# Layer 0's second context chunk as one 128-row operand; layer 1's normalisations on ScalarE with GpSimd's powers shared by two batches

## What is computed

```python
x = x + tanh(g_xattn[0]) * L0_xattn(ctx, layernorm(x), mask, ...)   # 4 heads of 64, keys from context and latents
x = x + tanh(g_ffn[0])   * L0_ffn(layernorm(x), ...)                # 8 experts, the best 2, and a shared one
x = x + tanh(g_xattn[1]) * L1_xattn(layernorm(x), ctx, ctx, ...)    # one head of 256
x = x + tanh(g_ffn[1])   * L1_ffn(layernorm(x), ...)                # 8 experts, the best 1
# L0_xattn: kv = concat([layernorm(ctx) @ Wkv.T, layernorm(latents) @ Wlkv.T]); softmax(q k) v @ Wo.T + bo
# L1_xattn: softmax((x Wq + bq) (ctx Wk + bk)^T) (ctx Wv + bv)
```

## Time and profile before

| | us |
|---|---|
| median of 3 runs | 1222.96 |
| lowest and highest run | 1221.63, 1227.02 |
| the profiled execution: its own time | 1228.26 |
| its span, first to last instruction | 1226.5 |

### The profile page before, as it was taken

The page is one execution under the profiler, slowest core; times in us unless marked ns, Lnnn a source line. Parts: engine busy times, 40 slices in busy tenths (PEclk is TensorE's granted clock), DMA queues, the critical chain, the costliest instruction groups (busy, mean ns, idle before and its releaser), DMA issues. The chain is left out here.

```text
span 1226.5 us, 30069 instructions
## 1 busy us (share of the span) xinstructions
PE 1052.9 (86%) x8055; PEld 811.7 (66%) x8056; DVE 742.9 (61%) x2369; ACT 568.7 (46%) x1310; POOL 449.0 (37%) x549
## 2 busy tenths in 40 slices
PE   3899999999999971999999999956878888179996
PEld 2687777777777751777777777745666767146664
DVE  5467777777777755344444443334788887445664
ACT  3466666666666640444444444422444444023332
POOL 3445666566665533000000000014577674312222
PEclk9799999999999975999999999977999999589999
DMA  4113221122211112354444443333743331444441
GB/s 135 32 36 107 78 70 57 60 74 76 83 57 45 46 69 86 87 129 126 126 125 128 128 99 83 84 97 109 232 137 119 102 119 52 121 98 105 111 111 50
DMA packets 153537, 116.26 MB, mean 95 GB/s; under 512 B 87695, under 2 KB 141249, under 8 KB 153218
## 3 DMA queue, kind: packets, MB, share of 16 engines
q1 hardware_dynamic: 112082, 57.46, 17.8%
q10 hardware_dynamic: 30816, 28.63, 7.9%
q0 software_dynamic: 10576, 29.41, 7.0%
HBM read 51.82 MB, written 45.92 MB: 80 GB/s over the span
## 5 line engine op out<-in xcount | busy, mean ns | idle before, releaser
L1458 PE MATMUL e_first<-w_high,e_z_cols 128*128 x824 | 175.4, 315 | 20.9 <-DMA e_z_cols<-z_rows 20.5
L1557 DVE SCALAR_TENSOR_TENSOR e_hidden<-e_first,e_act_out 128x352 f32<-128x352 f32 x103 | 54.0, 524 | 165.4 <-ACT e_act_out L1503 165.4
L1189 PE MATMUL a_out<-a_v_ones,a_probs 128*128 128x65 f32 x1024 | 140.2, 281 | 0.0
L1189 PEld LDWEIGHTS a_out<-a_v_ones,a_probs 128*128 128x128 f32 x1024 | 126.5, 194 | 15.1 <-issue 15.1
L1674 POOL IOTA a_first_numbers<- 128x2 int32 x1 | 0.1, 124 | 339.8 <-POOLq L70 339.8
L522 POOL DMA_INDIRECT z_rows<-r_z_halves,r_slot_idx x96 | 96.5, 1005 | 65.9 <-issue 32.7
L1458 PEld LDWEIGHTS e_first<-w_high,e_z_cols 128*128 128x128 f16 x824 | 81.0, 98 | 56.9 <-issue 21.3
L1562 DVE TENSOR_TENSOR e_hidden_low<-e_hidden_cols,e_hidden_high 128x384 f16<-128x384 f32 (+1 forms) x142 | 84.2, 593 | 48.9 <-ACT e_hidden_high L1512 48.2
L831 ACT ACTIVATE a_probs<-a_scores,a_latent_bias,a_k_scales 128x256 f32<-128x256 f32 x128 | 65.4, 561 | 99.5 <-PE a_scores L1175 62.1
L1503 ACT ACTIVATE e_act_out<-e_first 128x352 f32<-128x352 f32 x103 | 47.8, 464 | 136.2 <-PE e_first L1458 136.2
L1458 PE MATMUL e_first<-w_low,e_z_cols 128*128 x412 | 96.0, 315 | 0.0
(11 more groups left out here) (335 smaller groups left out, 2818.7 us busy)
## 6 DMA issues: line engine op xcount, KB each, us to landing
y_rows<-e_y_rows ACTq DMA_DIRECT2D x103, 128.0 KB, 1.7
w_stage<-in_v ACTq DMA_DIRECT2D x64, 128.0 KB, 2.3
w_stage_first<-in_w SPq DMA_DIRECT2D x18, 352.0 KB
a_ctx_in<-in_ctx SPq DMA_DIRECT2D x32, 192.0 KB, 3.2
e_token_rows<-z_rows ACTq DMA_DIRECT2D x39, 129.0 KB, 2.3
residual<-in_x SPq DMA_DIRECT2D x16, 256.0 KB, 3.0
z_rows<-r_z_halves SPq DMA_DIRECT2D x16, 256.0 KB, 2.2
a_y_shared<-y_rows SPq DMA_DIRECT2D x16, 256.0 KB, 2.9
```

Of the source, the lines that this page charges most:

```text
L1189: ins = pe.matmul(O[t][:, h * (D + 1):(h + 1) * (D + 1)], pm[x][:, jt, t * P:(t + 1) * P], va[p][:, jt, h, :], start=i + x == 0, stop=i + ...
L1458: ins = pe.matmul(GU[p][f][:, 0:F], x[z][:, k, :], w[:, ds(off, F)], start=(k == 0 and x is xh and w is wh), stop=(k == KC - 1 and x is xl))
L1557: v.scalar_tensor_tensor(hs[p][:], GU[p][1][:, 0:F], 1.0 / WSCALE, act_out[:], ALU.mult, ALU.mult).then_inc(hidden_done, 1)
```

## The change

**Layer 0.** The second context chunk (64 rows) becomes an operand of 128 rows. Rows 0 to 63 of `cTs[0]` hold the high half of the context, rows 64 to 127 its low half; `front_ctx_low` writes the latter there. The high weights of the chunk (`wcs[0]`) stand twice, one below the other; the low weights (`wcs[1]`) stand above zeros. Two passes (`CTX_PASSES`) then give what three gave. A copy on ScalarE and a memset on VectorE fill the new rows once.

**Layer 1, attention.** `z = x * rstd + shift`, with shift = -mean * rstd, is made on ScalarE (`act_z`), and so is the normalisation ahead of the attention (`pre_norm`). VectorE puts variance + eps and -mean of both batches in halves of the tiles `var` and `nmean`; GpSimd (`norms`) makes one power over four columns for batches n+2 and n-1 and one product for the shifts. `act_z(n-1)` hence waits for `norms(n)`, which waits for VectorE's `x2_mean_var(n+2)`. The low half of z moves from GpSimd to VectorE (`vector_z_low`), laid between the links of `vector_slots`; so are the two instructions of `x3(n)`. The gathers are fetched one batch earlier. PE's transposes are split (`turn_ctx`, `turn_x`) and `turn_x(n+1)` comes behind `score(n)`. The router's columns `zT` get a second buffer.

```diff
@@ phase_attn0 @@
+        CTX_PASSES = [(0, x, w) for x, w in PASSES] + [(1, 0, 0), (1, 0, 1)]
+                act.activation(wcs[0][NS1:P, 1, :], wc[0:NS1, 1, :], ACT.Copy, scale=WSCALE).then_inc(w_high, 1)
...
+                    v.wait_ge(w_high, len(split) + 1)
+                    v.memset(wcs[1][NS1:P, 1, :], 0.0).then_inc(w_low, 1)
...
                 def front_ctx_low(m):
                     v.wait_ge(s1_high, 2 * m + 2)
-                    for k, (o, w) in enumerate(CTX_CHUNKS):
-                        ins = v.tensor_tensor(cTs[1][0:w, k, :], cT[0:w, k, :], cTs[0][0:w, k, :], ALU.subtract)
-                    ins.then_inc(s1_low, 1)
+                    v.tensor_tensor(cTs[1][:, 0, :], cT[:, 0, :], cTs[0][:, 0, :], ALU.subtract)
+                    v.tensor_tensor(cTs[0][NS1:P, 1, :], cT[0:NS1, 1, :], cTs[0][0:NS1, 1, :], ALU.subtract).then_inc(s1_low, 1)
...
-                    for k, (o, r) in enumerate(CTX_CHUNKS):
-                        for x, w in PASSES:
-                            pe.matmul(bank[:, 0:S], wcs[w][0:r, k, i * P:(i + 1) * P], cTs[x][0:r, k, :], start=k + x + w == 0, stop=k == 1 and x == 1)
+                    for k, x, w in CTX_PASSES:
+                        pe.matmul(bank[:, 0:S], wcs[w][:, k, i * P:(i + 1) * P], cTs[x][:, k, :], start=k + x + w == 0, stop=k + w == 2)
...
@@ phase_attn1, GpSimd @@
+                def norms(n):
+                    ch = Chain(pool, p1, n + 2)
+                    lo, hi = 0 if within(n + 2, B) else T, 2 * T if within(n - 1, B) else T
+                    if lo == 0:
+                        pool.wait_ge(s1_stats, n + 3)
+                        pool.wait_ge(s1_norm, count(n + 2))
+                    if hi > T:
+                        pool.wait_ge(rt.stats_ready, n)
+                        pool.wait_ge(rt.z_ready, count(n - 1))
+                    ch.link(pool.tensor_tensor(rstd[:, lo:hi], var[:, lo:hi], g["mhalf"][:, lo:hi], ALU.pow))
+                    pool.tensor_tensor(shift[:, lo:hi], nmean[:, lo:hi], rstd[:, lo:hi], ALU.mult).then_inc(norm_ready, 1)
...
@@ phase_attn1, ScalarE's step @@
                     if core:
                         exps(n)
+                    if tail:
+                        act.wait_ge(norm_ready, n + 3)
+                        rt.act_z(act, n - 1, XRTile(g["XR"], n - 1), rstd[:, T:2 * T], shift[:, T:2 * T])
                     if front:
                         bias_q(n + 1, 1 - q)
                     if core:
                         prob_columns(n)
+                    if tail:
+                        rt.act_z_high(act, n - 1, 1 - q, False)
                     if within(n - 2, B):
                         rt.act_exp(act, n - 2)
...
+                    if within(n + 2, B):
+                        pre_norm(n + 2)
...
@@ phase_attn1, VectorE @@
-                def x2_mean_var():
+                def x2_mean_var(m):
...
+                    v.tensor_scalar(var[:, 0:T], mv[:, :, 1], EPS, None, ALU.add)
+                    v.tensor_scalar(nmean[:, 0:T], mv[:, :, 0], -1.0, None, ALU.mult).then_inc(s1_stats, 1)
...
-                    if tail:
-                        rt.vector_z(v, m, XRTile(g["XR"], m))
...
+                    def beside_slots(i):
+                        if tail and i < T:
+                            rt.vector_z_low(v, m, 1 - q, i)
+                        elif core and 3 <= i < 3 + T:
+                            x3(n, i - 3)
...
-                    if within(n + 2, B):
-                        pre_norm(n + 2)
```

More of the change, by code:

```diff
@@ L309, in __init__ @@
         self.st = sb("stats", [P, T, 6])
-        self.rstd = sb("rstd", [P, T])
+        if K == 2:
+            self.rstd = sb("rstd", [P, T])
         self.L = sb("logits", [P, T, E])
@@ L327, in __init__ @@
         self.zhalf = [halves(p) for p in range(2)]
-        self.zT = sb("z_cols", [P, KC, S])
+        self.zT = [sb(f"z_cols{p}", [P, KC, S]) for p in range(3 - K)]
         self.stats_ready = sem("stats_ready")
@@ L370, in vector_stats @@
         v.sem_inc(self.g["carried_v"], 1)
+        if self.K == 1:
+            for t in range(T):
+                ch.mark(v.bn_aggr(self.mv[:, t, :], self.st[:, t, :]))
+            ch.wait()
+            return
         for t in range(T):
@@ L383, in vector_z, with act_z, vector_z_low @@
         ins.then_inc(self.z_ready, 1)
+    def act_z(self, act, n, x, rstd, shift):
+        act.wait_ge(self.z_turned, count(n))
+        act.wait_ge(self.z_low, count(n))
+        act.sem_inc(self.g["carried_a"], 1)
+        for t in range(T):
+            ins = act.activation(self.z[:, t, :], x[:, t, :], ACT.Identity, bias=shift[:, t:t + 1], scale=rstd[:, t:t + 1])
+        ins.then_inc(self.z_ready, 1)
+    def vector_z_low(self, v, n, p, t):
+        v.wait_ge(self.z_high, n + 1)
+        ins = v.tensor_tensor(self.zhalf[p][t][:, C:2 * C], self.z[:, t, :], self.zhalf[p][t][:, 0:C], ALU.subtract)
+        if t == T - 1:
+            ins.then_inc(self.z_low, 1)
     def act_z_high(self, act, n, p, shared):
@@ L417, in pe_logits @@
             for k in range(KC):
-                ins = pe.matmul(bank[:, t, :], self.zT[:, k, t * P:(t + 1) * P], self.wg[:, k, :], start=k == 0, stop=k == KC - 1)
+                ins = pe.matmul(bank[:, t, :], self.zT[p % len(self.zT)][:, k, t * P:(t + 1) * P], self.wg[:, k, :], start=k == 0, stop=k == KC - 1)
         ins.then_inc(self.logits_ready, 1)
@@ L1131, in project_v_ctx @@
                     for t in range(T):
-                        for k, (o, r) in enumerate(CTX_CHUNKS):
-                            for x, w in PASSES:
-                                ins = pe.matmul(RB[1][:, t * C:(t + 1) * C], cTs[x][0:r, k, t * P:(t + 1) * P], wcs[w][0:r, k, C:2 * C],
-                                                start=k + x + w == 0, stop=k == 1 and x == 1)
+                        for k, x, w in CTX_PASSES:
+                            ins = pe.matmul(RB[1][:, t * C:(t + 1) * C], cTs[x][:, k, t * P:(t + 1) * P], wcs[w][:, k, C:2 * C],
+                                            start=k + x + w == 0, stop=k + w == 2)
                     ins.then_inc(proj_ready, 1)
@@ L1607, in phase_attn1 @@
         cin = [sb(f"ctx_in{p}", [P, T, DC]) for p in range(2)]
-        st, mv, r1 = sb("stats", [P, T, 6]), sb("mean_var", [P, T, 2]), sb("rstd", [P, T])
+        st, mv = sb("stats", [P, T, 6]), sb("mean_var", [P, T, 2])
+        var, nmean, rstd, shift = (sb(f"norm_{x}", [P, 2 * T]) for x in ("variance", "minus_mean", "rstd", "shift"))
         xn = sb("x_norm", [P, T, C])
@@ L1719, in joint_weights, with pre_norm, ctx_columns, x_columns @@
                     ins.then_inc(joint_ready, 1)
-                def columns(m, p):
-                    act.wait_ge(proj_ready, count(2 * m))
+                def pre_norm(m):
+                    act.wait_ge(s1_turned, count(m))
+                    act.wait_ge(norm_ready, m + 1)
+                    act.sem_inc(g["carried_a"], 1)
+                    x = XRTile(g["XR"], m)
+                    for t in range(T):
+                        ins = act.activation(xn[:, t, :], x[:, t, :], ACT.Identity, bias=shift[:, t:t + 1], scale=rstd[:, t:t + 1])
+                    ins.then_inc(s1_norm, 1)
+                def ctx_columns(m, p):
                     act.wait_ge(scored, count(m - 1))
-                    act.wait_ge(s1_turned, m + 1)
-                    act.activation(lT[:].rearrange("p k s -> p (k s)"), BT[:], ACT.Copy)
+                    act.wait_ge(proj_ready, count(2 * m - 2))
+                    act.wait_ge(s1_ctx_turned, m + 1)
                     for k, (o, w) in enumerate(CTX_CHUNKS):
                         ins = act.activation(cT[p][0:w, k, :], BC[0:w, k * S:(k + 1) * S], ACT.Copy)
-                    ins.then_inc(s1_cols, 1)
+                    ins.then_inc(s1_ctx_cols, 1)
+                def x_columns(m):
+                    act.wait_ge(proj_ready, count(2 * m))
+                    act.wait_ge(s1_turned, m + 1)
+                    act.activation(lT[:].rearrange("p k s -> p (k s)"), BT[:], ACT.Copy).then_inc(s1_cols, 1)
                 def bias_q(m, p):
@@ L1871, in step @@
                     m = n - 1
-                    if within(n + 3, B):
-                        slots(n + 3, 1 - q)
                     if core:
@@ L1877, in step @@
                         rt.vector_choose(v, n - 2, q, R[:, 0:T * E].rearrange("p (t e) -> p t e", t=T),
-                                         (lambda i: x2_step(n + 2, q, i)) if within(n + 2, B) else None)
+                                         (lambda i: x2_step(n + 2, q, i) if i < 7 else None) if within(n + 2, B) else None)
                     elif within(n + 2, B):
-                        for i in range(D1):
+                        for i in range(7):
                             x2_step(n + 2, q, i)
                     if within(n + 2, B):
-                        x2_mean_var()
-                    if tail:
-                        rt.vector_z(v, m, XRTile(g["XR"], m))
```

(3 more changed lines are left out.)

113 lines of the change are left out of this document (58 added, 55 removed).

## The result

The changed kernel takes 1269.5 us at the median of four runs (1268.9 to 1270.3), the kernel before, run beside it, 1222.6 (1221.6 to 1227.0). The ratio is 1.038, 95% interval 1.035 to 1.041: slower by 47 us, where 40 were forecast.

A forecast was written before the change was run, and what follows sets the result against it. PE was taken to bound attention 0, and a circle through several engines attention 1. Layer 1's +54 and layer 0's -14 gave +40 us on 1223, so 1263 us, range 1236 to 1290.

The forecast's parts named there:

- The circle in attention 1: Attention 1: a chain through several engines sets the step; it grows from 12.8 to 17.2 us, 4.4 more.
- A: Attention 1: the start of `x2_mean_var` on VectorE, from which each step is counted.
- The clock: Attention 1: PE's longer wait lowers its clock; products take 3.58 us, the step 17.2 against 15.8 at full clock.
- The rival with a low clock past the products: Attention 1: context, scores, tokens and logits also run low; 1302, or 1283 for half of the steps; 20%.
- T: Attention 1: the end of the products on PE, forecast to move from A + 3.43 to A + 7.0 at full clock.
- Half of the growth: Attention 1: full clock in every step and smaller hops, 15 us a step, 1236 us in all; 14%.
- The order on ScalarE at 1.4 us a step: Attention 1: `prob_columns` stands behind z and `bias_q` on ScalarE, which alone costs 1.4 us.
- Layer 1 at +54: Attention 1: 12 steps +53 us, n = 1 +4, the steps behind +1, the start -4; together +54.
- Layer 0 at -14: Attention 0: fewer passes spare PE 1.0 us a batch, 16 us in all, taken as 14, bounds 8 and 16.
- The rival "faster": Attention 1: VectorE's work sets the pace, so taking z and `pre_norm` off it gives 1185 us; 7%.

The follow-up runs named there:

- layer 1 alone: The changed kernel with just the layer 0 part undone, against the kernel before: ratio 1.044 (1.042 to 1.046), 54 us slower.
- layer 0 alone: The kernel before with all of the layer 0 part of the change and nothing of layer 1, against the kernel before: ratio 0.998 (0.995 to 1.000).
- z's own power: The changed kernel with GpSimd's power for z split off, waiting only for batch n-1's statistics, against the kernel before: 0.992, 1212.6 us.
- ScalarE's order undone as well: The changed kernel with a separate power for z, and bias_q and prob_columns ahead of z on ScalarE, against the kernel before: 0.986, 1204.8 us.

## Why the prediction was right, and where it was off

- **The circle in attention 1.** Right. z and PE's transposes wait for A. In the step shown, A to the end of the products was costed at 8.7 us and took 8.8, `x3` to the choice 4.1 and 4.0, choice to A 4.2 and 4.4; the mean step 17.2 against 17.1. PE's transposes stood at A + 4.7 by the sum and at A + 4.8 in the trace, the router's exponential was there at A + 5.5 and A + 5.6. Two pairs of errors cancel in this. z on ScalarE was costed at 0.71 us and took 1.09; shorter hops and links, and ScalarE's next instructions, which start before the last one ends, made up for most of it. And the slow products were costed at 3.58 and took 3.09, but the transposes ahead of them, costed at full clock (0.46), ran slow too (0.91). That part is luck.
- **The clock.** Right in both values: 17.2 with slow products and 15.8 without were costed, 17.1 and 15.4 measured. The granted clock was 0.80. The rule of the Trainium skill quoted there (TensorE: Matmul & The Clock Gate, "HAM oscillation — how this bites in real kernels"), that a burst behind such a wait starts slow, held in this trace: behind each of the twelve waits of 4.6 to 5.4 us the transposes took 1.11 us where filled waits gave 0.66.
- **The rival with a low clock past the products** (1283 to 1302) didn't come: the rows of the scores and of the logits behind them fit into the 4.2 us from T to the choice, and the granted clock from 960.8 to 965.0 was 1.00. Half of the growth (a step of 15 us, 1236) didn't come either: it needed full clock in every step.
- **The order on ScalarE at 1.4 us a step.** Its size was wrong as a price of its own: undone alone it gave 0.7 a step.
- **Layer 1 at +54.** 51.1 in the profile, 54 by the ratio of layer 1 alone. By its parts: from the fifth A (step n = 2) to the last it is eleven steps and +47.8 us, 4.35 each where 4.4 was costed; n = 1 +3.4 (4); from the last A to the end of the phase +7.5 (5.4); from the start of the phase to the fourth A -7.6 (-4). The last two miss in opposite directions and all but cancel, which again is luck; of the 7.6, some 3 show in the trace of layer 0 alone too, whose attention 1 is that of before.
- **Layer 0 at -14.** This step failed in size. The 0.30 us a group is exact (0.85 to 0.55), but "PE is the bound, and what it is spared is gained" held for the first 0.4 us a batch only, since a circle through VectorE lay just 0.4 us under PE's row. With about 14 batches that is 5 to 6 us; 3 to 6 were measured. The 8 us or more that are missing from the 14 are enough for the whole gap between 40 forecast and 47 measured. I had named ScalarE's exponentials as what might hold PE; it was VectorE's z.
- **The rival "faster"**, if VectorE's work set the pace: it was to decide if the way from A to `x3` stayed short. With z's own power it is 5.0 us on average over the ten full steps, and 4.2 with ScalarE's order undone as well, against 4.5 before; the kernels take 1213 and 1205 us. That this is VectorE's lighter row isn't shown: from the start of attention 1 to the fourth A it takes 40.7 and 40.6 us against 48.0 before, the twelve steps from there 152.7 and 144.6 against 153.1. So with its own power alone the steps are no shorter than before, and with the order too they are 0.7 us shorter each; what of that comes from VectorE wasn't tried apart.

## What to carry to other kernels

Before merging two small operations to save one, ask what each of them waited for: the merged one waits for the later of both inputs, and here 0.6 us of GpSimd time saved a step (two powers and two products of two columns take 1.85 us, one of each with four columns 1.23) put 30 us of handoffs into the circle and 21 more by the clock that fell in the longer wait. A nearly full engine (97%) says that it binds now, not how far the next circle lies beneath; add up the other engines' way around before counting a saving in full. Test a suspected circle by leaving out an instruction of it in both kernels: the same instruction was worth nothing in one and 0.4 us a batch in the other.

## What wasn't expected of the hardware

- The two ScalarE instructions that write z (256 f32 columns, scale and bias from memory) took 1.09 us, where two of the same width with f16 output took 0.71.
- An order that ends a wait sooner can meet a lower clock: the products took 3.62 us behind a wait of 4.08, 3.09 behind one of 5.19. In the changed kernel itself they took 3.62 us behind a wait of 4.81 and 2.87 behind one of 5.34. Which of the two it will be I can't derive from these rows.
- Filling PE's wait with 10 unneeded matmuls in the full steps made the changed kernel 21 us faster (1269.5 to 1248.7), and with 16 of them, or also in the last steps, most or all of that was lost again.
